# Seventy-eight further idle products on TensorE in the first front of a four-stage megakernel

## What is computed

```python
x = L0(x, A_grid, B_grid, dt)            # first and second differences, f + df*dt, maximum with 0
# L1: adapter
hidden = gelu(x @ down_W.T + down_b)     # 256 -> 64
hidden = hidden @ expert_W[id].T + expert_b[id] + domain_emb[id]
x = layernorm(hidden @ up_W.T + up_b + x) * ln_gamma + ln_beta
# L2: two rounds of a layer norm over the whole 256 x 256 sequence
y = silu(scale * (norm(x) * gamma + beta) + shift);  z = y @ W_in + b_in
y = silu(scale * (norm(z) * gamma + beta) + shift);  x = y @ W_out + b_out + x
# L3: encoder layer, 16 heads of 16
x = ln(x) * (1 + scale) + shift
q, k, v = x @ Wq + bq, x @ Wk + bk, x @ Wv + bv
x = x + softmax(q k^T / 4 + attention_bias, masked) v @ Wo + bo
x = x + gelu2((ln(x) * g2 + beta2) @ W1 + b1) @ W2 + b2
```

## Time and profile before

| | |
|---|---|
| median of three executions | 942.91 us (939.43 to 943.63) |
| profiled execution, its own time | 944.48 us |
| its span | 942.4 us |
| busy in the span: PE, DVE, ACT, POOL | 860.5, 725.7, 729.9, 235.2 us |
| mean granted TensorE clock | 0.967 of full speed |
| idle products | 58 (50 at the start, 8 before w_in(0)) |

### The profile page before, as it was taken

The page is one execution under the profiler, slowest core; times in us unless marked ns, Lnnn a source line. Parts: engine busy times, 40 slices in busy tenths (PEclk is TensorE's granted clock), DMA queues, the critical chain, the costliest instruction groups (busy, mean ns, idle before and its releaser), DMA issues.

```text
span 942.4 us, 18070 instructions
## 1 busy us (share of the span) xinstructions
PE 860.5 (91%) x5631; PEld 661.0 (70%) x5715; DVE 725.7 (77%) x2375; ACT 729.9 (77%) x1901; POOL 235.2 (25%) x236
## 2 busy tenths in 40 slices
PE   7676879999999999999999989999999999999987
PEld 6444656777777777777777777777777777777666
DVE  7655888898798878898787878898798878865432
ACT  3222978979798878979798878979798878978663
POOL 1332113332114313332113313332214313230100
PEclk9776899999999999999999999999999999999999
DMA  9814645553538353653537363553637363555500
GB/s 258 244 48 102 183 129 141 158 153 113 155 102 212 97 167 101 160 166 107 156 104 210 97 167 103 159 165 97 168 102 212 99 166 101 150 165 164 139 12 23
DMA packets 133081, 130.88 MB, mean 139 GB/s; under 512 B 18265, under 2 KB 123481, under 8 KB 132969
## 3 DMA queue, kind: packets, MB, share of 16 engines
q1 hardware_dynamic: 101072, 111.49, 42.4%
q10 hardware_dynamic: 31914, 18.23, 6.8%
HBM read 112.61 MB, written 17.07 MB: 138 GB/s over the span
## 4 chain that ended last, share of the span: by engine, by line
PE 52%; ACT 22%; DVE 9%; issue 5%; ACTq 0%; POOL 0%; DVEq 0%
PE ff_ps L1336 10%; PE ff_ps L1317 9%; PE PT_ps L1372 7%; ACT Pr L1059 6%; ACT L1059 4%; PE scores_ps L1357 4%; PE G L1141 4%; PE ctx_ps L1394 3%; PE scores_ps L1354 2%; PE ff_ps L1303 2%; ACT ffT L1045 2%; ACT PT L1072 2%; ACT tanh L1041 2%; PE G L1133 2%; DVE bias L923 2%
## 5 line engine op out<-in xcount | busy, mean ns | idle before, releaser
L1059 ACT ACTIVATE Pr<-bias,nmax 128x256 f32<-128x256 f32 x512 | 255.6, 505 | 53.6 <-DVE nmax L923 53.0
L923 DVE CUSTOM_DVE_ANT_0 bias<-scores_ps,bias 128x256 f32<-128x256 f32 x512 | 193.8, 419 | 38.7 <-issue 25.7
L1072 ACT ACTIVATE PT<-PT_ps 128x512 f32<-128x512 f32 x256 | 151.8, 593 | 43.9 <-PE PT_ps L1372 21.8
L1372 PE MATMUL PT_ps<-ident,Pr 128*128 128x128 f32 x1024 | 155.9, 274 | 9.2 <-ACT Pr L1059 9.2
L558 POOL TENSOR_TENSOR rstd<-var,half_neg 128x2 f32<-128x2 f32 (+1 forms) x64 | 42.7, 667 | 403.1 <-DVE var L682 264.9
L1372 PEld LDWEIGHTS PT_ps<-ident,Pr 128*128 128x128 f32 x1024 | 119.7, 141 | 18.4 <-ACT Pr L1059 14.6
L1317 PE MATMUL ff_ps<-ctxT,w 128*128 128x256 f32 x480 | 119.4, 392 | 14.0 <-ACT ffT L1045 9.9
L1336 PE MATMUL ff_ps<-w,ffT 128*128 128x256 f32 x480 | 114.2, 381 | 6.8 <-DVE ffT L900 6.8
L1317 PEld LDWEIGHTS ff_ps<-ctxT,w 128*128 128x128 f32 x480 | 87.8, 192 | 36.3 <-ACT ffT L1045 15.2
L1357 PE MATMUL scores_ps<-k_stack,q_stack 96*128 96x256 bf16 x512 | 99.4, 275 | 9.0 <-issue 4.3
L1059 ACT ACTIVATION_READ_ACCUMULATOR Pr<-bias,nmax 128x1 f32 x512 | 100.0, 195 | 0.0
(11 more groups left out here) (218 smaller groups left out, 1606.4 us busy)
## 6 DMA issues: line engine op xcount, KB each, us to landing
bias<-in_fside_Bx16xSxS_dram SPq DMA_DIRECT2D x256, 256.0 KB, 3.1
part_dram<-front ACTq DMA_DIRECT2D x32, 384.0 KB, 2.7
q_stack<-part_dram SPq DMA_DIRECT2D x32, 192.0 KB, 3.4
k_stack<-part_dram SPq DMA_DIRECT2D x32, 192.0 KB, 4.0
F<-in_x_dram SPq DMA_DIRECT2D x16, 256.0 KB, 3.8
ada<-rows_dram SPq DMA_DIRECT2D x16, 256.0 KB, 5.3
q_stack<-part_dram SPq DMA_DIRECT2D x32, 128.0 KB, 3.5
k_stack<-part_dram SPq DMA_DIRECT2D x32, 128.0 KB, 4.0
```

The costliest lines, as they stand in the source:

```text
L923: nc.vector.tensor_tensor_reduce(out=t, in0=SP_[:, n % 2, q * S:(q + 1) * S], in1=t, scale=-1.0, scalar=BIG, op0=ALU.add, op1=ALU.min, acc ...
L1059: ins = nc.scalar.activation(Pr[:, n % PR, q, :], bias[:, n // CH % RING, 2 * (n % CH) + q, :], ACT.Exp, bias=nmax[:, n, q:q + 1], scale=-1.0,
L1072: nc.scalar.activation(PT[:, m % BATCH, :, :].rearrange("p c q -> p (c q)"), TP[:, m % 2, :], ACT.Identity).then_inc(pt_ok, 1)
L1372: ins = pe.transpose(TP[:, m % 2, c * S + q * P:c * S + (q + 1) * P], Pr[:, m % PR, q, c * P:(c + 1) * P], ident[:, :])
```

## The change

The table WARM gets eight further entries, and three calls of `warm` are added on TensorE, for the first pair alone (`if not later(j)`); the calls for avg1 and q, and for w_in(1), were already in the code with a count of zero. The products are the same as before. In all, 16 + 4 + 10 + 3 + 6 + 5 + 20 + 14 = 78 are added. Each batch stands right before the wait of the step it is named after. No other engine's program changes.

```diff
-WARM = {"begin": 50, ("w_in", 0): 8}
+WARM = {"begin": 50, ("w_in", 0): 8, ("avg1", 0): 16, ("down", 1): 4, ("expert", 1): 10, ("up", 1): 3, ("q", 0): 6,
+        ("k", 0): 5, ("w_in", 1): 20, ("avg1", 1): 14}
...
                 for b in seqs("down", j, n):
+                    if not later(j):
+                        warm(("down", b))
                     pe.wait_ge(x1T_ok, 2 * j + b + 1)
...
                 for b in seqs("expert", j, n):
+                    if not later(j):
+                        warm(("expert", b))
                     pe.wait_ge(hid_ok, 2 * j + b + 1)
...
                 for b in seqs("up", j, n):
+                    if not later(j):
+                        warm(("up", b))
                     pe.wait_ge(expT_ok, 2 * j + b + 1)
...
                 for b in seqs("k", j, n):
+                    if not later(j):
+                        warm(("k", b))
                     pe.wait_ge(qk_ok[0], 2 * j + b + 1)
```

## The result

| | before | after |
|---|---|---|
| median, 20 executions each | 943.24 us (936.37 to 945.52) | 938.13 us (936.15 to 941.48) |
| ratio of the two, 95% interval | | 0.9953 (0.9942 to 0.9963) |
| profiled execution: own time, span | 944.48, 942.4 us | 941.48, 939.4 us |
| mean granted clock in it | 0.967 | 0.983 |
| first scores in it | 93.2 us | 89.3 us |

The profiled execution of the change is the slowest of its twenty, so its times are read for what follows what, and less for how much in all.

A forecast was written before the change was run, and what follows sets the result against it. TensorE's work bounds the steady part, so only its start could move: full clock in the first front, less overruns, brings the first scores 4.05 us earlier, rounded to 4.1, giving 938.8 us from the median of 942.91; range 935.5 to 943.0.

The forecast's parts named there:

- What can move is the time at which the steady part begins: TensorE's work bounds the steady part, busy 94.9 of 100 us; only its start, after the first front, can move.
- The condition of the forecast: First front: TensorE was assumed at full clock from 47.3 us to the first scores, the forecast's one condition.
- the first six overruns: Batches from avg1(0) to k(0) exceed their pauses by 1.25, 0.20, 0.40, 0.14, 0.23 and 0.19 us.
- The bound of -5.0: Sum if each batch costs nothing beyond its pause: -4.05 - 0.20 - 0.40 - 0.14 - 0.23 us.
- The terms behind k(0): DVE's split of k begins at 75.13 us, 4.05 earlier; store, SP's wait and load follow, scores at 89.2.
- Store, SP's wait, load and first scores follow with unchanged lengths: After DVE's split of k(0), the chain keeps its lengths, so the first scores come 4.05 us earlier, at 89.2.
- this batch's excess is hidden by the DMA: The 14 products before avg1(1) overrun by 0.80 us, covered because scores come 1.3 us behind avg1(1).
- The fall at 54.1 us: Clock fell after a pause of 2.32 us ended at 52.66; TensorE then worked 6.8 us at half clock.
- More is gained: Rival: w_out(1) also at full clock, 1.99 instead of 3.75 us; -5.9 in all, 937.0 us; chance 0.22.
- The clock falls once more: Rival: another fall between 54 and 78 us loses up to 3.4 us; about -1, 941.9 us; chance 0.16.
- The gain is lost behind the first scores: Rival: another wait, the bias-tile ring or second front, absorbs the gain; 942.9 us, no change; chance 0.08.
- Slower, because the products don't hold the clock: Rival: half clock from x1_turn(1) to k(0), products overrun their pauses; +7.4 us, 950.3 us; chance 0.06.

The follow-up runs named there:

- e4: The change with all 78 products made 32x32 pieces of the array over 256 columns; 979.71 us, ratio 1.0396 to before.
- e6: The change's eight places with counts fitted to end before each wait, 56 products instead of 78; 935.56 us, ratio 0.9926 to before.
- e10: All eight places with half of the fitted counts, 28 products added to the kernel before; 937.29 us, ratio 0.9934 to before.
- e1: Only the 16 products before avg1(0) added to the kernel before; 939.67 us, ratio 0.9970 to before.
- e9: The fitted counts at the first six places only, 32 products, none before w_in(1) and avg1(1); 937.66 us, ratio 0.9941 to before.
- e3: Only the 34 products before w_in(1) and avg1(1) added to the kernel before; 941.47 us, ratio 0.9987 to before.
- e5: The change with all 78 products made 32x32 pieces over 128 columns; 944.77 us, ratio 1.0038 to before.
- e8: The change plus 36 products in the pauses of 20 to 45 us, 114 in all; 936.13 us, ratio 0.9938 to before.
- e11: Every pause up to w_out(1) filled by fitted counts, 110 products added to the kernel before; 935.19 us, ratio 0.9916 to before.
- e12: The fitted 56 products with 22 in place of 10 before avg1(0), 62 in all; 938.57 us, ratio 0.9948 to before.

## Why the prediction was right, and where it wasn't

**The bound and the path to the end.** "What can move is the time at which the steady part begins": held in all fourteen kernels, to within 3.4 us in 848; e4, which moved it by 35 us, is the strong case.

**The condition of the forecast**, full clock from 47.3 to the first scores: in the profiled execution it held from 51.2 on. The length of each step at full clock, taken from the second front, was right to 0.1 us for q, k, up, w_in and w_out.

**The overruns.** The price of 0.223 us a product was right: the 32 records of the batch of 16 took 3.73 us. Less 0.27 for one record that is 31 steps of 0.112 us, as planned. What I did not draw from it is that the sum of the first six overruns, 2.4 us, was more than half of the gain forecast, and could be had by taking products away. The bound of -5.0, "if each batch costs nothing beyond its pause", took back those before down, expert, up and q and left out the 1.25 of the first; with it the sum is -6.3, and e6 measured -7.0 (5.9 to 8.1). I assumed that a pause has to be filled to its end; e10 did as well with 28 of the change's 78.

**The terms behind k(0).** DVE's split of k(0) began at 76.70 instead of the 75.13 forecast, without a wait for ScalarE, as forecast. The 1.6 us are the late start of this execution: its avg1(0) began 3.35 us later than before, of which 1.25 are the batch of 16. From avg1(0) to the split it is 20.7 us, where I had 75.13 - 53.9 = 21.2. The failed step is the next one: "Store, SP's wait, load and first scores follow with unchanged lengths". The store had 4.8 us in my one trace and 2.8 otherwise. With it fell "this batch's excess is hidden by the DMA": in the change it isn't (88.97 and then 89.33, no wait). SP's issue of the first stacked k also took longer, and the trace doesn't tell its 0.9 us from the lateness of avg1(1):

```profile
83.18 2.29 SPq L465 DMA_DIRECT2D k_stack<-part_dram  x3
```

Before it took 1.35 us. That the profiled first scores stand at 89.3, where 89.2 was forecast, is luck: the split came 1.6 late, the store was 2.0 shorter, and from load to scores it was 7.45 us instead of 6.84.

That the median was met all the same has a better reason. With the 849 us behind the first scores, before's median of 943.24 (a span of 941.1) puts the first scores of its typical execution near 92.1, an estimate. In the trace of before, avg1(1) at 91.67 would have let them go near 92.5 without the slow store (from avg1(1) to them it is 0.8 us at half clock in e1). So the path that mattered was most likely the one through w_in(1). The forecast had both paths some 4 us earlier (-4.05 and -3.83), and so came out right for either.

**The fall at 54.1 us.** The forecast read in one trace that the fall came 1.4 us after a pause of 2.32 us, and took that pause for its cause. The measurement speaks for this reading: filling pauses of 0.5 to 2.3 us brought 5.6 us (e9), and 7.0 with the one of 3.3 before w_in(1) (e6). How much of a stretch is at half clock differed from one execution of a program to the next, as in e3's one at 936.86 us (mean clock 0.982) against its others at 940 to 943 (0.974 to 0.978). Why, no run shows. I had read one execution of before as if its pattern were the program's.

**The rivals.** *More is gained* (w_out(1) at full clock, -5.9): w_out(1) did run in 1.97 us in place of 3.75, and it brought nothing that can be seen. It ran in 1.96 or 1.97 in four traces (the change, e5, e8, e11) and in 3.4 to 3.8 in the ten others, and span less first scores is 848.6 on average in the four, 848.8 in the ten. From 90.0 to 99.7 us DVE is busy 9.39 of 9.70, which fits the argument against it. *The clock falls once more*: not in the profiled execution, whose mean clock is 0.983. The other nineteen have 0.981 to 0.987, and a fall of 6.8 us is worth 0.004, so none had much more of the half clock than this one. *The gain is lost behind the first scores*: excluded by the same column: the change has 850.1, before 849.2, so at most 1 of 4 us went. *Slower, because the products don't hold the clock*: the products of the change do. e5 is what the rival would look like: batches of the same length, 1/16 of the array, 3.6 us slower than before.

**The size.** -4.1 was forecast and -4.4 (-3.5 to -5.5) measured, just inside the bound of 0.5%, for which the forecast had 0.56.

## What to carry to other kernels

Look at the granted clock of the stretch behind a pause, not only at the pause. Here one of 2.32 us stood before 6.8 us at 0.50, and q, in the half clock further on, took 3.78 us instead of 1.99. Where the clock falls behind pauses like this, fill them with work that loads the array: batches of 128x128 products brought 4.4 us (the change), batches of 32x32 pieces of the same length cost 3.6 (e5). Never put in more than fits: twelve products past a wait cost 2.1 us (e12 against e6), and half of a filling (e10, 6.2 us faster than before) did no worse than the overfilling of the change (4.4). And take the length of a DMA (2.8 or 4.8 us from store to load) and the pattern of the clock (a mean of 0.963 to 0.978 in one program) from several executions before building a sum on them.

## What the runs showed of the hardware

- One program, one input: the stretches at half clock differ between executions. Over the 66 executions of before that ran beside the experiments, the mean granted clock ran from 0.963 to 0.978 and the time from 937.24 to 946.15 us.
- With 32x32 fp32 pieces in place of 128x128 products of the same length (batches of 3.68 and 3.73 us) the clock was held less often: the twelve executions of e5 have a mean clock of 0.968 to 0.983 and took 940 to 953 us, the twenty of the change 0.981 to 0.987 and 936 to 941. In e4, with TensorE busy for 17.1 us without a gap, partly with such pieces, the granted clock stayed at 0.50 throughout.
- At the full clock 32x32 pieces of 128 columns at one place of the array are 0.11 us apart (e5: 3.68 us for 32, less 0.27, in 31 steps), as far as 128x128 products of 128 columns (0.112). Those of 256 columns are about 0.22 apart (estimate from e4: 8.63 us for 32, of which 3.2 at half clock).
- The same store of 384 KB to DRAM let the next load go after 4.8 us in one profiled execution (before) and after 2.8 us in the other thirteen. Why is open.
